# Two PSUM tiles for the expert gather, and eleven bisection rounds instead of twelve, in a fused attention and mixture-of-experts kernel

## The reference

```
# attention, for every batch row
dots = einsum('bhij,hk->bkij', q @ k^T * scale, pre_proj)   # heads mixed
dots = where(causal, neg, dots)
vk   = top_k(dots, 64)[..., -1:]                            # 64th largest of a row
attn = softmax(where(dots < vk, neg, dots))
s    = (einsum('bhij,hk->bkij', attn, post_proj) @ v) @ Wo + bo
# experts
scores = softmax(xn @ gate_w^T); topk_w, topk_idx = top_k(scores^T, cap)
x_tok  = xn[topk_idx]
eo     = (gelu(x_tok @ Wg^T) * (x_tok @ Wu^T)) @ Wd^T * topk_w
g      = silu(scatter_add(eo, topk_idx) + shared_expert(xn))
```

## Time and profile before

| | |
|---|---|
| median of 3 executions | 35060.98 us (35055.51 to 35069.14) |
| the profiled execution | 35062.15 us |
| its span (slowest core, core 5) | 35060.5 us |
| spans of the eight cores | 35025.9 to 35060.5 us |
| granted TensorE clock, every core | 1.0 |
| busy share of the span | TensorE matmul 45%, weight load 13%, DVE 26%, ScalarE 23%, GpSimd 1% |

### The profile page before, as it was taken

How to read it: one execution, slowest core, us unless ns; L and a number is a source line. 1 busy time by engine, 2 the same in 40 slices (tenths; PEclk the granted TensorE clock), 3 DMA queues, 4 the chain that set the end, 5 groups by cost and what they waited for, 6 DMA issues and landing times.

```text
span 35060.5 us, 208364 instructions; the slowest of 8 cores (35025.9 to 35060.5 us)
## 1 busy us (share of the span) xinstructions
PE 15835.9 (45%) x42800; PEld 4403.0 (13%) x42800; DVE 8979.0 (26%) x18561; ACT 8032.7 (23%) x15147; POOL 525.8 (1%) x703
## 2 busy tenths in 40 slices
PE   1377777776667775233223332235323233333332
PEld 0011111111111111011111111011101011111111
DVE  3300000000000001433433334431243433333444
ACT  1000000000110002432333333331332423333333
POOL 0000000000000000000000000000000000000000
DMA  1222222221001012000000000002100000000000
GB/s 37 57 36 36 36 36 36 36 36 37 31 23 32 16 20 35 4 4 4 2 2 2 4 2 0 2 2 28 16 4 4 2 4 2 2 2 2 2 2 1
DMA packets 499146, 565.26 MB, mean 16 GB/s; under 512 B 255202, under 2 KB 337266, under 8 KB 498034
## 3 DMA queue, kind: packets, MB, share of 16 engines
q0 software_dynamic: 346736, 392.38, 6.6%
q1 hardware_dynamic: 151298, 159.55, 1.5%
HBM read 709.30 MB, written 109.05 MB: 23 GB/s over the span
## 4 chain that ended last, share of the span: by engine, by line
PE 46%; DVE 21%; issue 21%; ACT 8%; DMA 3%; DVEq 1%; ACTq 0%; SPq 0%; another core or an unknown queue 0%; POOL 0%; POOLq 0%
DVE sb_csb L1401 12%; PE ps_xps L679 4%; PE ps_ovp L1529 4%; PE ps_dtp L1286 4%; PE ps_dps L762 3%; PE ps_acc L855 3%; PE ps_ups L723 3%; PE ps_gps L707 3%; DVE sb_pkb L1325 3%; PE ps_pkp L1316 3%; DVE sb_xrow L1465 2%; ACT sb_scr L1296 2%; ACT sb_xrow L1445 2%; PE ps_sacc L993 2%; PE ps_sus L963 2%
## 5 line engine op out<-in xcount | busy, mean ns | idle before, releaser
L1401 DVE TENSOR_SCALAR_CACHE_REDUCE sb_csb<-sb_xrow,sb_bst 128x256 bf16<-128x256 bf16 (+15 forms) x3072 | 4543.7, 1479 | 412.6 <-DVE sb_csb L1401 71.7
L1413 ACT ACTIVATE sb_csb<-sb_xrow,sb_bst 128x256 bf16<-128x256 bf16 (+15 forms) x3072 | 4021.3, 1309 | 1198.2 <-DVE sb_bst L1390 940.6
L1498 PE MATMUL ps_pm<-sb_patgs,sb_xrow 128*128 128x128 bf16 x2432 | 649.2, 267 | 7938.1 <-DVE sb_patgs L1481 7665.7
L1325 DVE COPY sb_pkb<-ps_pkp 128x128 bf16<-128x128 bf16 x4864 | 1091.2, 224 | 8381.9 <-PE ps_pkp L1316 8381.9
L1316 PE MATMUL ps_pkp<-sb_identb,sb_scr 128*128 128x128 bf16 x4864 | 1385.0, 285 | 1650.6 <-DVE sb_pkb L1325 1518.8
L679 PE MATMUL ps_xps<-sb_stl,sb_xn_tm 128*128 128x256 bf16 x4096 | 1519.5, 371 | 897.4 <-DMA sb_stl<-stm 164.0
L1286 PE MATMUL ps_dtp<-sb_qtl,sb_kbuf 64*128 64x128 bf16 x4864 | 1273.0, 262 | 1423.1 <-ACT sb_scr L1296 878.5
L1529 PE MATMUL ps_ovp<-sb_atb,sb_vT 128*64 128x128 bf16 x4864 | 1381.3, 284 | 969.0 <-DVE sb_atb L1509 288.0
L731 DVE TENSOR_TENSOR sb_hbuf<-sb_ggb,ps_ups 128x512 bf16<-128x512 f32 x256 | 175.9, 687 | 5087.2 <-PE ps_ups L723 5087.2
L762 PE MATMUL ps_dps<-sb_wdt,sb_hbuf 128*128 128x512 bf16 x2048 | 1196.8, 584 | 407.9 <-DVE sb_eo L769 121.1
L707 PE MATMUL ps_gps<-sb_xtok,sb_wgt 128*128 128x512 bf16 x2048 | 1208.1, 590 | 267.5
(11 more groups left out here) (163 smaller groups left out, 14856.7 us busy)
## 6 DMA issues: line engine op xcount, KB each, us to landing
sb_wgt<-wgT POOLq DMA_DIRECT2D x32, 2048.0 KB, 43.0
sb_wut<-wuT POOLq DMA_DIRECT2D x32, 2048.0 KB, 54.8
sb_wdt<-wdT POOLq DMA_DIRECT2D x32, 2048.0 KB, 65.0
stm<-sb_stb SPq DMA_DIRECT2D x32, 1024.0 KB, 6.1
sb_stl<-stm POOLq DMA_DIRECT2D x32, 1024.0 KB, 10.2
sb_sttb<-stm POOLq DMA_DIRECT2D x32, 1024.0 KB, 7.6
sb_ln_x<-x SPq DMA_DIRECT2D x32, 512.0 KB, 3.5
eo<-sb_eo POOLq DMA_DIRECT2D x128, 128.0 KB, 2.0
```

The lines of the kernel that those rows point to most:

```text
L1325: lambda v, si=si: v.tensor_copy(pkb[:, si * 128:si * 128 + 128], pkp[:, 0:128]),
L1401: v.tensor_scalar(sv, xrow[:, gl * JP:gl * JP + wjt], bcol(gl, 2), None, op0=ALU.is_ge, op1=ALU.add, accum_out=bcol(gl, 3)),
L1413: s.activation(sv, xrow[:, gl * JP:gl * JP + wjt], AF.Sign, bias=bcol(gl, 5), scale=1.0, accum_out=bcol(gl, 3)),
```

## The change

Two things change. The bisection has eleven rounds instead of twelve; the round that goes is the last, with the smallest step. And the gather writes alternately to two PSUM tiles, `xpsA` and `xpsB`, each of 512 fp32 columns (one bank), of which 256 are used. The first matmul of a group depends on the copy two groups back, `gb_prev[gpar]`, instead of the copy just before; the copies still depend on one another. `_gb_prev` is carried from expert to expert.

```diff
-    bis_sched: tuple = ("vector",) * 12
+    bis_sched: tuple = ("vector",) * 11
...
-            xps = self.ps("xps", [128, CAP], F32, esc)
+            xpsA = self.ps("xpsA", [128, 512], F32, esc)
+            xpsB = self.ps("xpsB", [128, 512], F32, esc)
...
+                gb_prev = getattr(self, "_gb_prev", [None, None])
                 for b in range(B):
                     for dt_ in range(DCH):
+                        gpar = dt_ % 2
+                        xv = xpsA if gpar == 0 else xpsB
...
-                                    xps[:, 0:CAP],
+                                    xv[:, 0:CAP],
...
-                                      gmm[-1] if gmm else prev_gather]))
+                                      gmm[-1] if gmm else gb_prev[gpar]]))
...
-                                xps[:, 0:CAP]),
+                                xv[:, 0:CAP]),
                             deps=[gmm[-1], prev_gather, prev_hh])
+                        gb_prev[gpar] = g_done[(b, dt_)]
                         prev_gather = g_done[(b, dt_)]
                     stl_use[b] = g_done[(b, DCH - 1)]
+                self._gb_prev = gb_prev
```

More of the change, by code:

```diff
@@ L677, in ph_experts @@
                             gmm.append(sc.step("tensor",
-                                lambda te, b=b, dt_=dt_, chk=chk:
+                                lambda te, b=b, dt_=dt_, chk=chk, xv=xv:
                                 te.matmul(
-                                    xps[:, 0:CAP],
+                                    xv[:, 0:CAP],
                                     self.xnt(b, chk)[:, dt_ * 128:
@@ L687, in ph_experts @@
                                       self.ln_done[0] if e == 0 else None,
-                                      gmm[-1] if gmm else prev_gather]))
+                                      gmm[-1] if gmm else gb_prev[gpar]]))
                         g_done[(b, dt_)] = sc.step("scalar",
-                            lambda s, b=b, dt_=dt_: s.copy(
+                            lambda s, b=b, dt_=dt_, xv=xv: s.copy(
                                 xtok[:, (dt_ * B + b) * CAP:
                                      (dt_ * B + b + 1) * CAP],
-                                xps[:, 0:CAP]),
+                                xv[:, 0:CAP]),
                             deps=[gmm[-1], prev_gather, prev_hh])
+                        gb_prev[gpar] = g_done[(b, dt_)]
                         prev_gather = g_done[(b, dt_)]
                     stl_use[b] = g_done[(b, DCH - 1)]
+                self._gb_prev = gb_prev
                 h_done = {}
```

## The result

The changed kernel takes 34402.91 us (median of 8 runs, 34396.68 to 34406.0), the kernel before 35061.31 us (8 runs): a ratio of 0.9812, 95% interval 0.9801 to 0.9822, 658 us or 1.9% less. The forecast was 34400 us.

The account below looks back on a forecast made before the run. The prediction took the kernel as a serial program with no one engine full, each operation costing its distance to the next. 464 + 197 = 661 us off gave 34400 us against the median, range 34365 to 34478 us after widening.

Parts of the forecast that it names:

- Term 1: Bisection: one steady round fewer in each of 32 tiles saves its whole start-to-start length, 464 us in all.
- Term 2: Gather: each of 240 changes of group costs 0.22 us instead of 1.04 with two tiles, saving 197 us.
- Cover: Gather: weight loads stay hidden, with over 50 us of room per expert, of which the shorter gather takes 12.
- (a): Rival, gather: a group's first matmul still pays a chained step of 0.52 us, gain 125 us, total 34472 us; 7%.
- (b): Rival, gather: no gain, the copy still ends each change or the loads end the stage; 34597 us; 3%.
- (c): Rival, bisection: the removed round's time is refilled by a wait it had covered; only the gather counts, 34864 us; 1%.
- (d): Rival, expert stage: alternating banks drops TensorE to its lower clock level, slower, 35920 us if only gather matmuls double; 2%.

Follow-up runs that it names:

- e2: The kernel before with eleven bisection rounds instead of twelve and its one gather tile: 34600.09 us, 464 us less than the kernel before.
- e5: The changed kernel with six bisection rounds instead of eleven: 32077.95 us, 2325 us less than the changed kernel.
- e1: The changed kernel with twelve bisection rounds, so only the two gather tiles are new: 34865.59 us, 198 us less than the kernel before.
- e3: The changed kernel, but a gather group's first matmul also waits for the last matmul of the group before: 34456.7 us, 54 us more than the changed kernel.
- e8: The kernel before with eleven rounds and one gather tile, every gather group copied twice from PSUM: 34683.85 us, 84 us more than e2.
- e4: The changed kernel with every gather group copied twice from PSUM on ScalarE: 34375.07 us, 28 us less than the changed kernel.
- e6: The changed kernel without the wait from matmul to matmul inside a gather group: 31954.0 us, 2449 us less than the changed kernel.
- e7: The changed kernel without any wait of TensorE for TensorE, except among the score matmuls: 23871.64 us, ratio 0.6817 to the kernel before.
- e10: The kernel before with eleven rounds and one gather tile, without waits from matmul to matmul inside a gather group: 32085.53 us, 132 us more than e6.
- e9: As e7, but with the one gather tile of before: 24016.12 us, 144 us more than e7.

## Why the prediction was right

- **Term 1, the round.** 464 us predicted, 464 measured in e2 and 465 a round in e5. The reading that made it exact was the distance from one line 1386 to the next, taken in a narrowest, a middle and a widest tile. DVE's busy time of the counts alone (379 us) would have been 85 us short. The wait of TensorE fell by 470 us, 6 more than the forecast; the last rounds of the 32 tiles, added up in the trace of before (core 5), are 465 us. What the other 5 us are was not looked into.
- **Term 2, the change of group.** 197 us predicted, 198 measured in e1, 195 between the traces, and the 8.02 us from group to group are the forecast's to the hundredth. That the free matmul behind a gather matmul costs 0.22 us and not a chained step of 0.52 was read from the one place where the old trace had it; e3 shows that the other value would have been wrong by 70 us, and e8 that the copy was paid in full.
- **Cover.** The weight loads stayed hidden, and a doubled copy cost the gather nothing (e4). The room that I had read at the end of the loads (over 50 us) is just used up in e6 (waits of 0.5 and 1.7 us for the up weights on cores 5 and 1) and gone in e7.
- **The rivals.** (a) falls by e3, which is rival (a) built and differs from the changed kernel, (b) by e1, (c) by e5.
- **Luck.** That the total came within 3 us is closer than the method is: the forecast's own range was 45 us wide, and the routing stage alone can move a kernel by 30 us. The slowest core had the long routing stage in the traces of before and after, so it dropped out.
- **What was wrong beside it.** Rival (d) and the sentences on the clock took the granted clock of 1.00 in the windows as the upper level. It was not. In e6, where the trace records the level, stretches marked 0.50 have the same 590 ns for a chained matmul of 512 columns as the changed kernel has where its clock reads 1.000 (e6 at 9000 to 9500 us, its window and its group by line, then the changed kernel):

```profile
9000.00:9500.00 500.00, 395.04 (x696) 72.54 (x696) 30.24 (x44) 31.34 (x47) 0.00 (x0) 0.50 0.06 21
L969 PE MATMUL ps_sus<-sb_xnfmb,sb_wsu 128*128 128x512 bf16 x221 | 130.3, 590 | 29.0
```

```profile
L729 PE MATMUL ps_ups<-sb_xtok,sb_wut 128*128 128x512 bf16 x2048 | 1208.1, 590 | 267.5
```

No matmul of 512 columns on core 5 of either kernel is shorter than 582 ns, where e6 has 376 ns at the upper level (the same line 729). And from the first scatter matmul to the end core 5 takes 26127 us in e6, all of it recorded at 0.50, and 26117 us in the changed kernel. So both kernels run TensorE at the lower level from end to end, and there was nothing to fall from: (d) could not have happened. Where it could have, in the gather of e6, TensorE alternates between the same two banks and keeps the upper level to the end of the gather. The Trainium skill's rule for back-to-back starts (TensorE: Matmul & The Clock Gate, "Wait — 56ns, not 53.3ns?") gives 0.21 us for 256 columns at 1.2 GHz and 0.11 us at 2.4 GHz. The traces agree at both levels, with 0.22 us in the earlier trace rows and 0.11 us in the third group of e6. I had the sentence and did not follow it to its end: what the upper level would be worth was missing from the theories of e6 and e7, and both were forecast too slow.

## What to carry to other kernels

In a serial program, price a removed operation by the distance from its start to the next start, not by its duration, and look for the step that will stand in its place somewhere in the old trace. A second PSUM tile saves the copy's wait plus the chained step that goes with it, once for each change of group (here 0.82 us), and no more; if the matmuls inside the group wait for one another, that is where the time is (2.4 ms in e6 against 0.2 ms for the second tile; taking such waits out of the whole program, e7, gives 10.5 ms on top of the change). A granted clock of 1.00 in a trace whose clock never changes says nothing of the level and is to be checked against the step of two free matmuls.

## What the runs showed of the hardware that I had not expected

- The level of TensorE: gather matmuls without gaps reach the upper level within two groups (e6), and a pause of 0.66 us behind every 1.9 us of work does not lose it (e10). Chained matmuls of 512 columns, 0.49 us apart, keep it through the gate and up matmuls. It goes among the down matmuls: on core 5 of e6 the second expert's begin at 1978.8 us, TensorE waits 1.08 us for DVE at 1987 us, and the record has the fall at 1988.2 us. In the one expert of core 1 where the up weights were late, it went at the beginning of the gate and up matmuls, inside the 1.69 us wait. Both falls lie at a wait, but nothing was built to show that the wait is the cause, and the chained matmuls before it may have a part in it.
- The routing stage, whose code only e7 and e9 touch, takes different times on different cores of the same execution. The 32 stores of the one-hot matrix (1 MB each) land in a median of 5.0 us on core 0 of the changed kernel and 6.1 us on core 7 (columns: KB each, us to landing):

```profile
stm<-sb_stb SPq DMA_DIRECT2D x32, 1024.0 KB, 5.0
```

```profile
stm<-sb_stb SPq DMA_DIRECT2D x32, 1024.0 KB, 6.1
```

  From the first routing load to the first gather matmul it is 1011 and 1040 us. In e3, e4 and e8 all eight cores have the short length, in the profile of the kernel before all have the long one, in e5 cores 0 and 1 the long and the others the short. Cores 4 and 5 of the changed kernel lie between (1029 and 1025 us): their stores follow each other 13.9 us apart at first and 14.9 us apart from the middle of the stage on. In every trace here the two cores of a pair (0 and 1, 2 and 3, and so on) go alike. Since the slowest core sets the time, this moves a kernel by up to 30 us with nothing of its own changed; in the traces it is the 28 us of e4. What decides it stays open: no run here separates the place of the buffers in memory from what the neighbouring cores do.
